# Rotary embedding turned in place in PSUM for the first three tiles of a decoder layer

## The chip, the cores and the metric

The kernel runs on one core of one Trainium2 chip. The metric is the device time of one execution in microseconds (us), smaller is better. TensorE (PE, with its weight loads as PEld), VectorE (DVE), ScalarE (ACT) and GpSimd (POOL) each run their own queue of instructions; SyncE (SP) issues most of the DMAs. Engines order themselves against each other with semaphores. SBUF holds operands, PSUM (8 banks of 512 float32 in each of 128 partitions) takes the results of TensorE. GpSimd works on SBUF alone in this kernel; VectorE and ScalarE work on both.

## The reference, cut to what matters

One pre-norm decoder layer on x of shape (2, 256, 512): causal self-attention with 32 query heads and 8 key/value heads of size 16, attention over a context, and a ternary feed-forward part. The change touches the rotation of queries and keys:

```python
def _apply_rope(x, cos, sin):
    x1, x2 = jnp.split(x, 2, axis=-1)
    return jnp.concatenate([x1 * c - x2 * s, x1 * s + x2 * c], axis=-1)

x = x + attn(layernorm(x))     # q = rope((x @ Wq) heads), k = rope((x @ Wk) heads), v = x @ Wv
x = x + cross_attn(layernorm(x), ctx)
x = x + bitlinear_ffn(layernorm(x))
```

## The kernel before, in words

The 512 tokens are four tiles t = 0..3 of 128 (two per batch element). For each tile TensorE multiplies the normalised, transposed tile with the joined weights: 512 columns of queries (e = 0) and 256 columns of keys and values (e = 1), each into a PSUM bank: `qkv_bank(t, e)` (L215) is banks 1, 2 for tile 0, banks 3, 4 for tile 1, banks 7, 4 for tile 2. Tile 3 is done later, among the attention steps, and goes through an SBUF place (`proj_place`, L365).

The attention scores are made from operands split into a high part (float32r, rounded by the write) and a low part (what is left over). So for each tile and each e:

- `rotate(t, e)` (L795, VectorE): L812 multiplies the projection with cos into the SBUF tensor `roped`; for e = 1, L815 copies the values to `vaug`; L819, twice, multiplies the swapped halves with the signed sin into `rope_tmp`; L823 adds `rope_tmp` to `roped`. The increment of `rope_read` on the second L819 is also what tells TensorE that the bank is free.
- `heads_high(t, e)` (L555, ScalarE, L565 for queries and L569 for keys): rounds `roped` into `stk`, twice per head.
- `heads_low(t, e)` (L825, VectorE, L832 and L835): `roped` minus the high part into `stk`.
- `stack_T` (L1152, TensorE, L1156): transposes `stk` in 5 stacks of 4 transposes per tile; the results for the tiles 0 and 1 go to banks 5, 1, 6, 2 in turn (`ST_BANKS`), so stack 1 overwrites the queries of tile 0 and stack 3 its keys. ScalarE copies them out (L576).

The order on each engine is written out by hand. VectorE (L862 to L883): low part of the transposed tile 1 (L841), rotate(0,0), a small shift for tile 3 (`mean_shift(3)`, L851), rotate(0,1), the low parts of tile 0, `tile_low(2)`, rotate(1,0), rotate(1,1), `tile_low(3)`, the low parts of tile 1, a small product (L876), rotate(2,0), rotate(2,1), low parts of tile 2, then the attention loop (L1067). ScalarE (L723 to L742): ..., `tile_T(1)`, heads_high(0,0), `normalise(3)` (L716), heads_high(0,1), tile_T(2), tile_T(3), copies of the stacks 0 to 4, heads_high(1, ...), copies of the stacks 5 to 9, heads_high(2, ...). TensorE (L1341 to L1357): the projections of tiles 0 and 1, the last passes of tile 1 with the low part of the weights (L1144), `tile_T(3)` (L1110, needs normalise(3)), stacks(0), the queries of tile 2, stacks(1), the keys of tile 2. GpSimd makes the low part of the weights meanwhile (L496, two SBUF inputs, four instructions) and then a chain of products for the context attention (L513, L515, L518).

From about 29 us the loop over 16 groups of heads runs (L1479 on TensorE, L1067 on VectorE): scores by query into banks 0, 1, 2, maxima on VectorE in place in PSUM (L1003), transposed maxima, scores by key, exp, causal select on GpSimd (L535), weighted values. Side work is put between by the table `BESIDE` (L285): "rot", "hi", "lo", "st" of tile 3, "whole" (L406, scaling of the feed-forward weights, shared by GpSimd and VectorE), "a" (L1205, L662 and L983) and so on.

## Time and profile before

| | |
|---|---|
| median of 3 runs | 230.72 us (230.19 to 231.79) |
| the profiled execution | 231.82 us, of which the span of the trace is 230.1 us |
| mean granted TensorE clock | 0.989 of full speed |
| PE busy | 213.2 us (93%) |
| DVE busy | 155.3 us (67%) |
| ACT busy | 124.8 us (54%) |
| POOL busy | 59.7 us (26%) |

The busy shares are taken over the whole span. In the first 35 us all five engines take part in one chain; in the feed-forward part at the end TensorE alone is nearly always busy. The page's fourth section gives the chain that ended last 67% on PE, 16% on DVE and 9% on ACT.

### The profile page before, as it was taken

What the parts mean: (1) busy time and instruction counts of PE and PEld (TensorE: products, weight loads), DVE (VectorE), ACT (ScalarE), POOL (GpSimd) and SP (SyncE); (2) the same over time, 40 slices, a digit from 0 to 9 for tenths busy, and PEclk for the clock granted to TensorE, in tenths of its full rate; (3) what the DMA queues carried; (4) which work ended last, traced back from release to release, by engine and by line L of the source; (5) the groups of instructions that cost most, each with busy time, mean ns of one, the idle gap of its engine ahead of it and who ended that gap; (6) DMA issues with size and microseconds to landing.
All of it is one profiled execution on the core that took longest, in us unless ns stands there. A gap on an engine that the chain in (4) does not pass through costs nothing.

```text
span 230.1 us, 4338 instructions
## 1 busy us (share of the span) xinstructions
PE 213.2 (93%) x1492; PEld 153.6 (67%) x1500; DVE 155.3 (67%) x567; ACT 124.8 (54%) x210; POOL 59.7 (26%) x76
## 2 busy tenths in 40 slices
PE   8898989979988899999899997999999999999993
PEld 3377867656765567456764544888987878767771
DVE  2489988997896897599922658888655675353233
ACT  2638768766699755558695645726524124322320
POOL 4499920473222438432201060000000010000000
PEclk9999999997999999999999999999999999999998
DMA  6999400000652121453701180000000000020002
GB/s 177 372 401 413 161 1 1 4 2 1 209 185 104 47 53 46 137 183 97 252 12 49 33 333 0 3 0 3 0 1 0 3 0 0 3 91 0 3 0 93
DMA packets 9079, 19.98 MB, mean 87 GB/s; under 512 B 1153, under 2 KB 1537, under 8 KB 9057
## 3 DMA queue, kind: packets, MB, share of 16 engines
q1 hardware_dynamic: 8480, 19.60, 24.4%
q8 instruction: 12, 0.20, 0.4%
q10 hardware_dynamic: 576, 0.10, 0.2%
q14 instruction: 11, 0.08, 0.1%
HBM read 18.58 MB, written 1.05 MB: 85 GB/s over the span
## 4 chain that ended last, share of the span: by engine, by line
PE 67%; DVE 16%; ACT 9%; issue 6%; DVEq 0%; POOL 0%; ACTq 0%; POOLq 0%
PE ps L1314 14%; PE ps L1177 10%; PE ps L1329 8%; DVE ps L1003 4%; PE ps L1205 4%; PE ps L1267 3%; PE ps L1236 3%; PE ps L1283 3%; PE ps L1338 3%; PE ps L1156 3%; PE ps L1110 2%; PE ps L1377 2%; PE ps L1459 2%; PE ps L1388 2%; PE ps L1418 2%
## 5 line engine op out<-in xcount | busy, mean ns | idle before, releaser
L1003 DVE CUSTOM_DVE_ANT_0 ps<-ps,maskf 128x128 f32<-128x128 f32 (+1 forms) x128 | 41.1, 392 | 1.1 <-PE ps L1388 0.9
L535 POOL TENSOR_SCALAR_AFFINE_SELECT prob<-prob 128x512 f32<-128x512 f32 x32 | 20.6, 666 | 67.5 <-ACT prob L750 67.5
L750 ACT ACTIVATE prob<-ps 128x1536 f32<-128x1536 f32 x16 | 23.3, 1453 | 20.1 <-PE ps L1424 20.1
L620 ACT CAST in_hi<-inter 128x256 f16<-128x256 f32 (+1 forms) x22 | 8.9, 405 | 24.0 <-DVE inter L956 24.0
L485 POOL TENSOR_TENSOR rstd<-veps,neghalf 128x1 f32<-128x1 f32 x12 | 6.6, 552 | 57.2 <-DVE veps L785 57.2
L1314 PE MATMUL ps<-h_hi,gate_q 128*128 128x256 f16 (+1 forms) x88 | 20.4, 273 | 0.0
L1314 PE MATMUL ps<-h_hi,up_q 128*128 128x256 f16 (+1 forms) x88 | 20.4, 273 | 0.0
L1314 PE MATMUL ps<-h_lo,up_q 128*128 128x256 f16 (+1 forms) x88 | 20.4, 272 | 0.0
L1314 PE MATMUL ps<-h_lo,gate_q 128*128 128x256 f16 (+1 forms) x88 | 20.4, 272 | 0.0
L956 DVE TENSOR_TENSOR inter<-gate_s,ps 128x256 f32<-128x256 f32 (+1 forms) x22 | 9.2, 419 | 14.8 <-PE ps L1314 14.3
L1003 DVE DVE_READ_ACCUMULATOR2_ANT mx<- 128x1 f32 x128 | 17.9, 140 | 0.0
L1329 PE MATMUL ps<-wqkv,in_lo 128*128 128x512 bf16 (+1 forms) x44 | 16.7, 379 | 0.8 <-DVE x L966 0.5
L613 ACT ACTIVATE gate_s<-ps 128x256 f32<-128x256 f32 (+1 forms) x22 | 8.4, 381 | 16.1 <-PE ps L1314 16.0
L1205 PE MATMUL ps<-xwk,xwq 128*128 128x256 f32 x64 | 16.2, 396 | 0.1
L959 DVE TENSOR_TENSOR in_lo<-inter,in_hi 128x256 f16<-128x256 f32 (+1 forms) x22 | 9.3, 425 | 10.4 <-ACT in_hi L620 10.4
L1205 PEld LDWEIGHTS ps<-xwk,xwq 128*128 128x128 f32 x64 | 11.7, 194 | 3.1 <-issue 1.1
L1329 PE MATMUL ps<-wqkv,in_hi 128*128 128x512 bf16 (+1 forms) x36 | 13.6, 379 | 0.0
L1377 PE MATMUL ps<-ksT,qsT 64*128 64x128 f32 x64 | 10.8, 289 | 3.0 <-DVE amat_lo L983 2.2
L1377 PEld LDWEIGHTS ps<-ksT,qsT 64*128 64x128 f32 x64 | 8.6, 188 | 6.6 <-issue 5.8
L1388 PE MATMUL ps<-ksT,qsT 64*128 64x256 f32 x64 | 12.3, 306 | 0.5 <-DVE mT L1073 0.3
L1156 PE MATMUL ps<-ident,stk 128*128 128x128 f32 x80 | 11.3, 278 | 1.2 <-ACT up_q L638 0.7
L1418 PE MATMUL ps<-qsT,ksT 64*128 64x512 f32 x32 | 11.7, 446 | 0.0
(185 smaller groups left out, 546.6 us busy)
## 6 DMA issues: line engine op xcount, KB each, us to landing
raw<-gate_dram SPq DMA_DIRECT2D x1, 2752.0 KB, 17.2
raw<-up_dram SPq DMA_DIRECT2D x4, 688.0 KB, 5.0
wqkv<-wqkv_dram SPq DMA_DIRECT2D x4, 384.0 KB, 6.1
raw<-down_dram SPq DMA_DIRECT2D x2, 768.0 KB, 4.7
x<-x_dram SPq DMA_DIRECT2D x4, 256.0 KB, 5.6
xwq<-xwq_dram SPq DMA_DIRECT2D x1, 1024.0 KB, 8.9
xwk<-xwk_dram SPq DMA_DIRECT2D x1, 1024.0 KB, 11.1
wo<-wo_dram SPq DMA_DIRECT2D x1, 1024.0 KB, 18.0
```

The lines of the kernel that those rows point to most:

```text
L535: nc.gpsimd.affine_select(out=v, in_=v, compare_op=ALU.is_ge, fill=0.0, base=0, pattern=[[0, GROUP], [1, P]], channel_multiplier=-1).then_ ...
L750: nc.scalar.activation(prob[:, i % 2, :], ps[:, 3:6, :].rearrange("p a b -> p (a b)"), ACT.Exp, scale=DH ** -0.5).then_inc(exp_done, 1)
L959: nc.vector.tensor_tensor(in_lo[0:r, n % 3, :], inter[0:r, n % 2, :], in_hi[0:r, n % 3, :], ALU.subtract).then_inc(in_lo_ready, 1)
L1003: nc.vector.tensor_tensor_reduce(scores, scores, mask, 1.0, LOWEST, ALU.add, ALU.max, to).then_inc(max_done, 1)
L1156: mm = nc.tensor.transpose(to[:, a * P:(a + 1) * P], stk[:, t % 2, h:h + 2, :, :].rearrange("p h c d -> p (h c d)"), ident[:, :])
L1177: mm = nc.tensor.matmul(to, lhs(k), rhs(k), start=(k == 0 and n == 0), stop=(k == KD - 1 and n == 2))
L1205: mm = nc.tensor.matmul(to[:, 0:T], xwq[:, k, m * P:(m + 1) * P], xwk[:, k, half * T:(half + 1) * T], start=(k == 0), stop=(k == KD - 1))
L1314: mm = nc.tensor.matmul(ps[0:r, where + n % 2, 0:T], w[:, k, cols], h[:, k, b * T:(b + 1) * T], start=(k == 0 and h is h_hi), stop=(k == K ...
L1329: mm = nc.tensor.matmul(bank(4 + q), half[0:r, n % 3, q * P:(q + 1) * P], down_q[0:r, it * D:(it + 1) * D], start=(it == 0 and half is in_hi),
L1377: nc.tensor.matmul(ps[:, 0, h * P:(h + 1) * P], qsT[b][rows, 4 * gp + h, 0:P], ksT[rows, gp, b * T:b * T + P], start=True, stop=True).then ...
L1388: nc.tensor.matmul(ps[:, 1 + h // 2, (h % 2) * T:(h % 2 + 1) * T], qsT[b][rows, 4 * gp + h, P:T], ksT[rows, gp, b * T:(b + 1) * T], start= ...
L1418: nc.tensor.matmul(bank(3 + n), ksT[rows, gp, b * T:b * T + P], qsT[b][rows, 4 * gp + 2 * n:4 * gp + 2 * n + 2, :], start=True, stop=True)
```

## The change

For the tiles 0 to 2 the projection is no longer moved to `roped`. VectorE first makes the two sin products into `rope_tmp` (SBUF), then multiplies the projection with cos in place in its PSUM bank, then adds `rope_tmp` in place in the bank. ScalarE rounds the high parts and VectorE takes the low parts from the bank. Tile 3 does the same in `proj_place`, in SBUF. The copy of the values comes after the cos product. The semaphore `rope_read` is gone: a bank is free once the low part is taken (`lo_ready`), and a new semaphore `turned` orders VectorE's own steps, with a wait before the cos product and one before the sum (before: one, ahead of the sum). The wait for an old `roped` buffer (`hi_ready`, t >= 2) is gone.

```diff
@@ -184,8 +184,8 @@
...
         w_high, w_low_done = sem("w_high"), sem("w_low_done")
-        qkv_ps, rope_read, roped_ready, v_sb = (
-            sem("qkv_ps"), sem("rope_read"), sem("roped_ready"), sem("v_sb"))
+        qkv_ps, turned, roped_ready, v_sb = (
+            sem("qkv_ps"), sem("turned"), sem("roped_ready"), sem("v_sb"))
         hi_ready, lo_ready = sem("hi_ready"), sem("lo_ready")
@@ -363,6 +363,12 @@
...
         proj_place = up_q[:, :, :].rearrange("p a b -> p (a b)").bitcast(F32)[:, 0:QK]
+
+        def rotated(t, e):
+
+            columns = slice(0, D) if e == 0 else slice(D, QK)
+            place = proj_place[:, columns] if t >= EARLY else qkv_bank(t, e)[:, 0:QK - D if e else D]
+            return place.rearrange("p (h d) -> p h d", d=DH)
@@ -559,15 +565,15 @@
...
                     act.wait_ge(stack_set, 4)
-                r = roped[:, t % 2, :].rearrange("p (h d) -> p h d", d=DH)
+                r = rotated(t, e)
                 s = stk[:, t % 2, :, :, :].bitcast(F32R)
...
                     nc.scalar.copy(s[:, 0:HEADS, 1:3, :],
-                                   r[:, 0:HEADS, :].unsqueeze(2).broadcast_to([P, HEADS, 2, DH])
+                                   r.unsqueeze(2).broadcast_to([P, HEADS, 2, DH])
                                    ).then_inc(hi_ready, 1)
...
                     nc.scalar.copy(s[:, HEADS:, 1:4:2, :],
-                                   r[:, HEADS:, :].unsqueeze(2).broadcast_to([P, KV, 2, DH])
+                                   r.unsqueeze(2).broadcast_to([P, KV, 2, DH])
                                    ).then_inc(hi_ready, 1)
@@ -584,7 +590,7 @@
...
                 if w == 1 and c == 0:
-                    act.wait_ge(rope_read, 2 * TT)
+                    act.wait_ge(lo_ready, 2 * TT)
                 nc.scalar.activation(tern_target(w)[0:rows, at:at + n], raw[0:rows, at:at + n], ACT.Abs,
@@ -803,36 +809,35 @@
...
                     src = proj_place[:, lo * DH:hi * DH]
-                if t >= 2:
-                    dve.wait_ge(hi_ready, 2 * (t - 2) + e + 1)
-                to = roped[:, t % 2, lo * DH:hi * DH]
+                src = src[:, 0:nh * DH]
                 tmp = rope_tmp[:, lo * DH:hi * DH]
-                halves = src[:, 0:nh * DH].rearrange("p (h e d) -> p h e d", e=2, d=DH // 2)
+                halves = src.rearrange("p (h e d) -> p h e d", e=2, d=DH // 2)
                 cos = rope[:, t % 2, 0, :].unsqueeze(1).broadcast_to([P, nh, DH])
-                nc.vector.tensor_tensor(to.rearrange("p (h d) -> p h d", d=DH),
-                                        src[:, 0:nh * DH].rearrange("p (h d) -> p h d", d=DH), cos, ALU.mult)
-                if e == 1 and t < EARLY:
-                    nc.vector.tensor_copy(vaug[:, t, :, 0:DH], src[:, nh * DH:nh * DH + KV * DH].rearrange(
-                        "p (h d) -> p h d", h=KV)).then_inc(v_sb, 1)
                 for half in range(2):
...
                                                   halves[:, :, 1 - half, :], sin, ALU.mult)
-                ins.then_inc(rope_read, 1)
-                dve.wait_ge(rope_read, 2 * t + e + 1)
-                nc.vector.tensor_tensor(to, to, tmp, ALU.add).then_inc(roped_ready, 1)
+                ins.then_inc(turned, 1)
+                dve.wait_ge(turned, 4 * t + 2 * e + 1)
+                heads = src.rearrange("p (h d) -> p h d", d=DH)
+                nc.vector.tensor_tensor(heads, heads, cos, ALU.mult).then_inc(turned, 1)
+                if e == 1 and t < EARLY:
+                    nc.vector.tensor_copy(vaug[:, t, :, 0:DH], qkv_bank(t, e)[:, nh * DH:nh * DH + KV * DH].rearrange(
+                        "p (h d) -> p h d", h=KV)).then_inc(v_sb, 1)
+                dve.wait_ge(turned, 4 * t + 2 * e + 2)
+                nc.vector.tensor_tensor(src, src, tmp, ALU.add).then_inc(roped_ready, 1)
...
                 dve.wait_ge(hi_ready, 2 * t + e + 1)
-                r = roped[:, t % 2, :].rearrange("p (h d) -> p h d", d=DH)
+                r = rotated(t, e)
                 s = stk[:, t % 2, :, :, :]
...
                 if e == 0:
-                    nc.vector.tensor_tensor(w[:, 0:HEADS, 3, :], r[:, 0:HEADS, :], s[:, 0:HEADS, 1, :],
+                    nc.vector.tensor_tensor(w[:, 0:HEADS, 3, :], r, s[:, 0:HEADS, 1, :],
                                             ALU.subtract).then_inc(lo_ready, 1)
                 else:
-                    nc.vector.tensor_tensor(w[:, HEADS:, 2, :], r[:, HEADS:, :], s[:, HEADS:, 1, :],
+                    nc.vector.tensor_tensor(w[:, HEADS:, 2, :], r, s[:, HEADS:, 1, :],
                                             ALU.subtract).then_inc(lo_ready, 1)
@@ -1163,9 +1168,8 @@
...
                     if s in (1, 3):
-                        pe.wait_ge(rope_read, 2)
                         pe.wait_ge(v_sb, 1)
-                    pe.wait_ge(lo_ready, 2 * t + 1 + (s % NST) // (NST - 1))
+                    pe.wait_ge(lo_ready, 2 if s == 3 else 2 * t + 1 + (s % NST) // (NST - 1))
                     if s >= len(ST_BANKS):
@@ -1352,14 +1356,14 @@
...
             stacks(1)
-            pe.wait_ge(rope_read, 4)
+            pe.wait_ge(lo_ready, 4)
             pe.wait_ge(v_sb, 2)
...
                     pe.wait_ge(xnT_low, TT - 1)
-                    pe.wait_ge(rope_read, 2)
+                    pe.wait_ge(lo_ready, 2)
                     pe.wait_ge(v_sb, 1)
@@ -1407,7 +1411,7 @@
...
                 if i == 0:
-                    pe.wait_ge(rope_read, 2 * EARLY)
+                    pe.wait_ge(lo_ready, 2 * EARLY)
                     pe.wait_ge(v_sb, EARLY)
```

## Rows read from the trace of the kernel before

**Rows 1.** Busy time by stretch: stretch, its length, each engine's busy us (instructions), granted clock

```profile
15.47:18.31 2.84, 2.84 (x20) 2.52 (x19) 2.84 (x2) 0.00 (x0) 2.84 (x4) 1.00 1.04 416
19.21:20.16 0.95, 0.00 (x1) 0.00 (x1) 0.90 (x2) 0.95 (x3) 0.95 (x2) 1.00 1.00 411
49.31:50.75 1.44, 0.00 (x1) 0.03 (x1) 1.44 (x4) 0.68 (x1) 0.83 (x1) 1.00 0.00 0
51.10:54.50 3.40, 3.40 (x28) 2.24 (x26) 2.80 (x19) 2.18 (x4) 0.66 (x2) 0.50 0.01 1
...
57.20:62.70 5.50, 5.26 (x46) 4.09 (x47) 4.96 (x25) 3.21 (x6) 1.22 (x2) 1.00 0.53 174
```

**Rows 2.** The chain that ended last, 11 to 31 us: start us, us, what

```profile
19.30 0.82 ACT xn L716
...
20.16 0.66 PE ps L1110 x4
20.82 2.37 PE ps L1156 x20
...
26.00 2.24 PE ps L1156 x20
```

**Rows 3.** VectorE in order of time: start us, us, line, out<-in, count

```profile
14.09 0.68 DVE L812 TENSOR_TENSOR roped<-ps,rope 128x512 f32<-128x512 f32 x1
14.69 0.75 DVE L819 TENSOR_TENSOR rope_tmp<-ps,rope 128x256 f32<-128x256 f32 x2
15.47 2.84 DVE L823 TENSOR_TENSOR roped<-roped,rope_tmp 128x512 f32<-128x512 f32 x1
...
22.90 0.69 DVE L823 TENSOR_TENSOR roped<-roped,rope_tmp 128x512 f32<-128x512 f32 x1
...
25.70 1.37 DVE L835 TENSOR_TENSOR stk<-roped,stk 128x128 fp32r<-128x128 f32 x1
```

**Rows 4.** GpSimd in order of time, the same columns

```profile
14.07 3.68 POOL L496 TENSOR_TENSOR w_lo<-wqkv,qsT 128x768 fp32r<-128x768 f32 x2
...
21.64 1.29 POOL L518 TENSOR_TENSOR bkq<-bkq,oT 128x512 f32<-128x512 f32 x1
...
25.11 1.81 POOL L518 TENSOR_TENSOR bkq<-bkq,oT 128x512 f32<-128x512 f32 x1
```

**Rows 5.** ScalarE in order of time, the same columns

```profile
18.34 1.05 ACT L565 CAST stk<-roped 128x1024 fp32r<-128x1024 f32 x1 [4.89 <-DVE roped L823]
```

**Rows 6.** VectorE by line and shape, 0 to 52 us: busy us, mean ns

```profile
L1003 DVE CUSTOM_DVE_ANT_0 ps<-ps,maskf 128x256 f32<-128x256 f32 x16 | 6.4, 459 | 0.0
...
L983 DVE TENSOR_TENSOR amat_lo<-ps,xnT_r 128x256 fp32r<-128x256 f32 x2 | 0.8, 417 | 0.4 <-ACT xnT_r L662 0.4
```

**Rows 7.** The chain that ended last, 34 to 52 us

```profile
50.20 0.42 DVE amat_lo L983
```

**Rows 8.** VectorE in order of time, 47 to 49 us

```profile
47.07 0.59 DVE L812 TENSOR_TENSOR roped<-up_q,rope 128x128 f32<-128x128 f32 x1
47.58 0.65 DVE L819 TENSOR_TENSOR rope_tmp<-up_q,rope 128x64 f32<-128x64 f32 x1
...
48.85 1.42 DVE L823 TENSOR_TENSOR roped<-roped,rope_tmp 128x128 f32<-128x128 f32 x1
```

**Rows 9.** GpSimd in order of time, 46 to 50 us

```profile
46.11 1.41 POOL L406 TENSOR_SCALAR raw<-raw,inv 128x1376 f32<-128x1376 f32 x1
...
47.48 0.68 POOL L535 TENSOR_SCALAR_AFFINE_SELECT prob<-prob 128x512 f32<-128x512 f32 x1
...
48.11 0.63 POOL L535 TENSOR_SCALAR_AFFINE_SELECT prob<-prob 128x512 f32<-128x512 f32 x1
48.73 1.41 POOL L406 TENSOR_SCALAR raw<-raw,inv 128x1376 f32<-128x1376 f32 x1
```

**Rows 10.** VectorE in order of time, 18 to 20 us

```profile
18.36 0.28 DVE L812 TENSOR_TENSOR roped<-ps,rope 128x128 f32<-128x128 f32 x1
...
19.12 0.29 DVE L823 TENSOR_TENSOR roped<-roped,rope_tmp 128x128 f32<-128x128 f32 x1
```

## The prediction, made before the changed kernel was run

> **What bounds the kernel now.** I read the table of busy time by stretch first, then the chain of waits, then the queues of VectorE, GpSimd and ScalarE side by side. The table shows a stretch of 2.84 us (15.47 to 18.31) in which VectorE has two instructions, ScalarE none at all, and TensorE still has work; a little later, 19.21 to 20.16, TensorE stands still for 0.95 us [rows 1]. The chain goes through both: the sum of rotate(0,0), then the normalisation of tile 3 on ScalarE, then TensorE's transpose of tile 3 at 20.16 and the stacks [rows 2]. Side by side the queues say why: the sum L823 on 512 columns takes 2.84 us at 15.47 and 0.69 us at 22.90 [rows 3]. During the long one GpSimd runs two L496 without a break, from 14.07 to 17.75 [rows 4]; 18.31 - 17.75 = 0.56 us is the sum's own work, so it made no headway before GpSimd stopped. Both read two tensors from SBUF. The cos and sin products at 14.09 and 14.69, with one input in PSUM, ran at 0.68 us and 0.75 us (for two) in the same GpSimd stretch [rows 3]. It comes again: L835, two SBUF inputs, takes 1.37 us at 25.70 where 128 columns take some 0.29 us [rows 3, 10]; GpSimd's L518 runs 25.11 to 26.92, and is itself 0.52 us over its 1.29 us because L832 came first [rows 4].
>
> The Trainium skill says this of it (SBUF — State Buffer, "Who interferes with whom"): a VectorE instruction with two SBUF inputs and a GpSimd instruction that reads SBUF lock each other out for a whole instruction, and one with at most one SBUF input does not contend. By that rule the trace agrees, with the 2.84 us beside 0.69 us above.
>
> **What is removed.** In the tiles 0 to 2 the sums and the low parts get one input from PSUM, so these stalls go: 2.84 - 0.69 = 2.15 us at 15.47 and 1.37 - 0.29 = 1.08 us at 25.70. Neither is worth its size on the path.
>
> The first. Rotate(0,0) becomes two sin products 0.75, cos product 0.68, sum 0.69, and 0.03 us at each of two waits (14.69 + 0.75 = 15.44, next start 15.47 [rows 3]): 14.09 + 2.18 = 16.27 us instead of 18.31. Then ScalarE's high part, 1.05 us [rows 5], and the normalisation, 0.82 us [rows 2]: tile 3 is normalised at about 18.2 us. But TensorE works until 19.21 on the last passes of tile 1, whose weights come from the same GpSimd instructions [rows 1], and these gain nothing. So of 2.0 us the path gets the 0.95 us in which TensorE stood still. Next due are the stacks: they need the low part of tile 0's queries, at about 17.4 + 0.7 = 18.1 us, and transpose 3 first, so TensorE decides and not they. A small part comes on top: in the chain the first 20 stack transposes take 2.37 us and the next, which do not wait for tile_low(2), 2.24 us [rows 2]. I take 0.1 us.
>
> The second, 1.08 us at 25.70, holds back rotate(2,0). Its result is wanted by ScalarE only after the stack copies of tile 1, and the keys of tile 2, which TensorE finishes later, decide when VectorE may start on the maxima. I cost it at nothing; the cover is over 1 us of TensorE's projection of those keys. If the cover were gone it would be worth up to 1.08 us, the lower bound of the range takes that in.
>
> **What is added.** One more wait per rotation. Before, the products overlapped (14.09 to 14.69 is 0.60 us for a 0.68 us instruction); now the cos product starts only when the sin products are through. That is 0.03 + 0.08, about 0.1 us each, eight times. Six lie before VectorE becomes the bound and are covered by the 2.0 us. The two of tile 3 lie on the path (the chain is VectorE's from 36 to 50 us): 0.1 us for the first; the second is hidden in the stall below, bound 0 to 0.1 us.
>
> In-place operation in PSUM with two inputs is nowhere shown for this line. Nearest: the maxima L1003, in place in PSUM, 459 ns for 256 columns, and L983, PSUM and SBUF into SBUF, 417 ns [rows 6]. So in place costs between nothing and 0.04 us per 256 columns, 0.08 us for 512; I take nothing, since 1 us of slack on VectorE hides six of these at either price. ScalarE reading its high part from PSUM: between 0 and 0.1 us of the 1.05, either way hidden by the same 1 us.
>
> The other page on this speaks against the change: VectorE: DVE Perf Modes, "The TRN2 errata", gives a VectorE instruction with a PSUM source 62 cycles more than one with an SBUF source, an estimate of 0.06 us each at its 0.96 GHz. The trace shows the opposite of a difference: 0.68 us from PSUM (L812) and 0.69 us from SBUF (L823 at 22.90) [rows 3]. By the page some 12 instructions would cost 0.8 us of VectorE, all under the slack, and the sum would be the same.
>
> Banks are held longer. Stack 3 now waits for both low parts of tile 0. The second is short behind the first (keys: 0.28 us for the product to 0.29 us for the sum [rows 10]) and behind ScalarE's normalisation; by my walk it is ready near 18.8 us, and stack 3 is due near 21.2. Bank 4 for tile 2's keys waits for the low part of tile 1's keys, which the tenth stack ahead of it in TensorE's queue waits for anyway. Cost nothing, with over 2 us of cover on the first. The waits on all eight low parts ahead of the up-weights come tens of us after their release.
>
> **The stall that stays.** Tile 3 is rotated in SBUF, before and after. At 47 us VectorE's four operations alternate with GpSimd's queue: L812 waits for the end of a L406 at 47.52, the first sin product (0.65 us for 64 columns) for a select until 48.16, the second for the next select, and the sum, 1.42 us, for a third L406 until 50.14 [rows 8, 9]. The next step in the chain starts at 50.20 [rows 7]; TensorE has nothing from 49.31 to 50.75, and then runs at a granted clock of 0.50 (1.2 GHz) for 3.4 us, 51.1 to 54.5 [rows 1]. That costs about 1 us: the step from 50.75 to 57.21 takes 6.46 us, the next, of nearly the same content, 5.5 us [rows 1]. In the new order it is again four operations in the same place, sin, sin, cos, sum. What decides is whether two sin products slip in between a L406 and a select. The nearest row is the pair itself: after the first select, one 64-column product got in and the second lost to the next select. So I take that the pattern stays, and the sum ends where it does now, within 0.05 us.
>
> **The sum**, against the profiled execution of 231.82 us (span 230.1): -0.95 - 0.1 + 0.1 + 0.0 = -0.95 us, so 230.87. It lies 1.10 us over the median of the runs, which the forecast is to be compared with: 230.72 - 0.95 = 229.8 us. From 50 us on nothing hangs on absolute time, the loads being issued behind the same steps, so I let the gain pass through to the end.
>
> **Rivals.**
>
> 1. *The stall at 47 us breaks too.* If the two sin products pass in one gap (64 columns instead of 128 end earlier), the sum comes before the third L406 and rotate(3,1) ends near 49.0 instead of 50.27: 1.3 us, no gap of 1.44 us on TensorE and, if the clock then holds, 1 us more. 229.8 - 2.3 = 227.5 us. For it: the margins are below 0.1 us. Against: the pair row above. Chance 0.23.
>
> 2. *The gain is given back.* The shifted work meets one more stretch at half clock (1 us as above) or the steps of the loop fall differently: 230.7 us. For it: the one stretch is set off by a gap that small shifts could make elsewhere; against: the 0.95 us gap did not lower the clock (1.00 in both rows), and gaps shrink. Chance 0.14.
>
> 3. *The change doesn't do what it says*: a sum in PSUM with one SBUF input is still held up by GpSimd. Then all stays, plus 0.2 us of added waits: 230.9 us. The products at 14.09 and 14.69 speak against it. Chance 0.04.
>
> 4. *Slower.* The added wait in the rotation of tile 3 lengthens TensorE's gap and with it the half clock in the loop. Every us of TensorE work at half clock costs about 1/3.4 = 0.3 us, so it decides against the 0.95 us gain only when over 3.2 us more are run so; at twice that, 229.8 + 1.9 = 231.7 us. Against it: the added time is 0.1 us on a gap of 1.44 us. Chance 0.07.
>
> The forecast itself has 0.52.
>
> **How the numbers follow.** 1% is 2.3 us, about what a measurement of this kernel tells from no change. Only rival 1 (227.5) and the lower edge of my own case pass 228.4: faster 0.23 + 0.02 = 0.25. Slower by over 1% means over 233.0 us, twice rival 4's loss: 0.05 of its 0.07. The rest is 0.70. The range reaches from rival 1 less 0.2 us, 227.3, to rivals 2 and 3 and a run's scatter, 231.1; the likeliest case alone is 229.0 to 230.5, the lower end with the 1.08 us above partly on the path, the upper with in-place costs and the waits of tile 3.
>
> **What would show it.** L823 at about 15.6 us at 0.7 us; L835 of tile 1 at 0.3 us; TensorE without its 0.95 us gap; the transpose of tile 3 near 19.3; the first maxima, L1003, about 1 us earlier than now; the sum of rotate(3,1) still 1.4 us and the half clock near 50 to 54. The forecast is wrong if the last two are gone, if GpSimd's L496 now take longer than 1.84 us each, or if a new low-clock stretch appears.

## The result: 229.61 us, and the profile of the changed kernel

| | before | changed |
|---|---|---|
| median (18 runs each) | 230.59 us | 229.61 us (228.49 to 230.25) |
| ratio, with its 95% interval | | 0.9949 (0.9931 to 0.9966) |
| the profiled execution, and its span | 231.82, 230.1 us | 229.55, 227.8 us |
| mean granted TensorE clock in it | 0.989 | 1.00 |

(One of the 18 runs of before was 533.26 us, the others 229.72 to 231.94; the median is not moved by it.) The change saves 1.0 us by the medians and 1.2 us by the ratio, whose interval is 0.8 to 1.6 us. The forecast was 0.95 us. Lines have moved: the sin products are L818, the cos product L823, the sum L828, the low parts L837 and L840, the dot product ahead of tile 2's rotation (L876 before) L881, the maxima L1008, the transposes of tile 3 L1115, the stacks L1161, the scores L1381.

VectorE of the changed kernel in order of time (start us, us, line, out<-in):

```profile
14.16 0.75 DVE L818 TENSOR_TENSOR rope_tmp<-ps,rope 128x256 f32<-128x256 f32 x2
14.94 0.70 DVE L823 TENSOR_TENSOR ps<-ps,rope 128x512 f32<-128x512 f32 x1
15.67 0.70 DVE L828 TENSOR_TENSOR ps<-ps,rope_tmp 128x512 f32<-128x512 f32 x1
...
24.31 0.28 DVE L840 TENSOR_TENSOR stk<-ps,stk 128x128 fp32r<-128x128 f32 x1
24.51 1.20 DVE L881 CUSTOM_DVE_ANT_0 stat<-bqk 128x4 f32<-128x4 f32 x1
```

GpSimd and ScalarE in the same stretch:

```profile
14.14 3.68 POOL L502 TENSOR_TENSOR w_lo<-wqkv,qsT 128x768 fp32r<-128x768 f32 x2
...
24.42 1.28 POOL L524 TENSOR_TENSOR bkq<-bkq,oT 128x512 f32<-128x512 f32 x1
```

```profile
16.41 1.02 ACT L571 CAST stk<-ps 128x1024 fp32r<-128x1024 f32 x1 [2.89 <-DVE ps L828]
17.31 0.82 ACT L722 ACTIVATE xn<-x,shift,rstd 128x512 f32<-128x512 f32 x1
```

GpSimd's two products take 3.68 us as before [rows 4], but the sum inside them now takes 0.70 us where it took 2.84 us [rows 3]. Rotate(0,0) ends at 16.37 us. The stall of 1.08 us at the low part L835 is gone too, but the dot product behind it, whose two inputs lie in SBUF, takes 1.20 us in place of 0.15 us: the stall moved to the next instruction with two SBUF inputs.

The chain that ended last, 17 to 29 us (start us, us, what):

```profile
17.86 1.39 PE ps L1149 x8
19.24 0.44 PE ps L1115 x4
19.68 2.18 PE ps L1161 x20
...
24.67 2.18 PE ps L1161 x20
...
28.25 0.63 PE ps L1381 x4
```

It is TensorE's alone from 8.75 us to the first scores, where before it went through VectorE's sum and ScalarE's normalisation [rows 2]. TensorE has no gap ahead of tile 3. Busy time by stretch (the stretch, its length, the busy us of PE, PEld, VectorE, ScalarE and GpSimd in this order, then the granted clock, the DMA share and GB/s):

```profile
48.12:49.54 1.42, 0.00 (x1) 0.03 (x1) 1.42 (x4) 0.67 (x1) 0.80 (x1) 1.00 0.00 0
49.54:55.02 5.48, 4.91 (x44) 3.62 (x44) 4.65 (x23) 3.17 (x6) 1.22 (x2) 1.00 0.00 1
56.00:61.50 5.50, 5.25 (x48) 4.10 (x46) 5.01 (x23) 3.87 (x5) 1.22 (x2) 1.00 0.67 238
```

The gap of TensorE ahead of 50 us is still there, 1.42 us for 1.44 [rows 1]. In this execution the half clock did not follow it: the step behind it took 5.48 us, at a granted clock of 1.00, where before it took 6.46 us. So the two profiles differ by more than the change: 230.1 - 227.8 = 2.3 us of span, of which 50.75 - 49.54 = 1.21 us was gained by 50 us, 6.46 - 5.48 = 0.98 us is the half-clock stretch, and 0.1 us lies later. The experiments must say whether that 0.98 us belongs to the change. The two traces start alike: GpSimd's pair of products begins at 14.07 us in one and at 14.14 us in the other.

### The profile page after: what moved, and what is told of

Same layout as the page of the kernel before. It is cut to its first block, busy times and chain, and to the rows that moved or that the text cites. A ratio compares the mean times of both kernels' runs of the same rounds, so it can differ in the third digit from the quotient of the medians.

```text
span 227.8 us, 4334 instructions
## 1 busy us (share of the span) xinstructions
PE 211.5 (93%) x1492; PEld 152.6 (67%) x1500; DVE 153.7 (67%) x567; ACT 124.7 (55%) x210; POOL 57.5 (25%) x76
## 3 DMA queue, kind: packets, MB, share of 16 engines
HBM read 18.58 MB, written 1.05 MB: 86 GB/s over the span
## 4 chain that ended last, share of the span: by engine, by line
PE 70%; DVE 16%; ACT 7%; issue 6%; DVEq 0%; POOL 0%; ACTq 0%; POOLq 0%
PE ps L1318 14%; PE ps L1181 10%; PE ps L1333 8%; DVE ps L1008 5%; PE ps L1271 3%; PE ps L1240 3%; PE ps L1287 3%; PE ps L1342 3%; PE ps L1161 3%; PE ps L1209 3%; PE ps L1115 3%; PE ps L1130 2%; PE ps L1381 2%; ACT prob L756 2%; PE ps L1140 2%
## 5 line engine op out<-in xcount | busy, mean ns | idle before, releaser
L1008 DVE CUSTOM_DVE_ANT_0 ps<-ps,maskf 128x128 f32<-128x128 f32 (+1 forms) x128 | 41.1, 392 | 0.7 <-PE ps L1392 0.6
L541 POOL TENSOR_SCALAR_AFFINE_SELECT prob<-prob 128x512 f32<-128x512 f32 x32 | 20.0, 649 | 67.2 <-ACT prob L756 67.2
L1008 DVE DVE_READ_ACCUMULATOR2_ANT mx<- 128x1 f32 x128 | 17.9, 140 | 0.0
L1381 PE MATMUL ps<-ksT,qsT 64*128 64x128 f32 x64 | 10.6, 285 | 2.8 <-DVE amat_lo L988 1.9
L1381 PEld LDWEIGHTS ps<-ksT,qsT 64*128 64x128 f32 x64 | 8.5, 186 | 6.3 <-issue 5.7
L1161 PE MATMUL ps<-ident,stk 128*128 128x128 f32 x80 | 11.1, 277 | 1.7 <-ACT up_q L644 0.7
L412 POOL TENSOR_SCALAR raw<-raw,inv 128x1376 f32<-128x1376 f32 (+1 forms) x8 | 11.2, 1407 | 1.8 <-DVE inv L896 1.8
```

The lines of the kernel that those rows point to most:

```text
L412: unit.tensor_scalar(v, v, inv[0:rows, w:w + 1], ROUND, ALU.mult, ALU.add).then_inc(pool_whole if unit is nc.gpsimd else dve_whole, 1)
L541: nc.gpsimd.affine_select(out=v, in_=v, compare_op=ALU.is_ge, fill=0.0, base=0, pattern=[[0, GROUP], [1, P]], channel_multiplier=-1).then_ ...
L1008: nc.vector.tensor_tensor_reduce(scores, scores, mask, 1.0, LOWEST, ALU.add, ALU.max, to).then_inc(max_done, 1)
L1161: mm = nc.tensor.transpose(to[:, a * P:(a + 1) * P], stk[:, t % 2, h:h + 2, :, :].rearrange("p h c d -> p (h c d)"), ident[:, :])
L1381: nc.tensor.matmul(ps[:, 0, h * P:(h + 1) * P], qsT[b][rows, 4 * gp + h, 0:P], ksT[rows, gp, b * T:b * T + P], start=True, stop=True).then ...
```

## The experiments

Theory A, that of the forecast: the sum of rotate(0,0) is what counts, 0.95 us and a little more, because TensorE is next; the rest of the change costs and brings nothing. Theory B: the half clock behind 50 us is part of the effect. Theory C: the gain comes from other places of the change (low parts, rotations of tile 1, the later release of the banks). Unless told otherwise, ratios are to the kernel before on the same chip, with their 95% interval; that kernel's median is 231.15 us (35 runs) beside experiments 1 to 4, 231.01 (22) beside 5 to 8, 230.63 (25) beside 9 to 12, which are three chips. For each execution the mean granted clock is known too. The profiled ones with a half-clock stretch of some 3.5 us have 0.989 to 0.993, so executions at 0.994 or less are counted as having one, and the others are called executions at full clock. At full clock the kernel before has 230.81, 230.79 and 230.33 us on the three chips.

### 1. The kernel before, unchanged

> The kernel before, unchanged, beside itself. Theory (the stretch at half clock near 51 us comes and goes from run to run and costs about 1 us): the runs fall in two groups about 1 us apart, near 230.3 and 231.5 us, and those with the longer time show a mean clock near 0.99, the others 1.00; ratio 1.000 within 0.003. Rival (the stretch belongs to every run of this kernel, and its end is what the change won): all runs near 231 us at a clock of 0.99.

231.64 us (230.05 to 232.64), ratio 1.0004 (0.9970 to 1.0037); 8 of the 12 executions have the lower mean clock. Its profile shows another course than the one that the prediction was made from. VectorE and GpSimd:

```profile
14.75 0.75 DVE L819 TENSOR_TENSOR rope_tmp<-ps,rope 128x256 f32<-128x256 f32 x2
15.53 1.00 DVE L823 TENSOR_TENSOR roped<-roped,rope_tmp 128x512 f32<-128x512 f32 x1
...
17.35 1.05 DVE L823 TENSOR_TENSOR roped<-roped,rope_tmp 128x128 f32<-128x128 f32 x1
...
22.74 1.08 DVE L823 TENSOR_TENSOR roped<-roped,rope_tmp 128x128 f32<-128x128 f32 x1
```

```profile
14.13 1.86 POOL L496 TENSOR_TENSOR w_lo<-wqkv,qsT 128x768 fp32r<-128x768 f32 x1
15.94 2.31 POOL L496 TENSOR_TENSOR w_lo<-wqkv,qsT 128x768 fp32r<-128x768 f32 x1
```

The sum starts 15.53 - 14.13 = 1.40 us behind GpSimd's pair, exactly as in the first profile (15.47 - 14.07 [rows 3, 4]). There it waited for the end of the pair and took 2.84 us. Here it took 1.00 us, of which 0.56 us are its own work (as in the prediction), so it waited 0.44 us, until 15.97 us. That is the seam of the pair (14.13 + 1.86 = 15.99 us). At the seam the waiting sum was let in, and GpSimd's second product took 2.31 us for the 1.86 us of the first. In the first profile the sum had waited as long when the seam came, and GpSimd's second product was let in ahead of it: the same encounter at the same distance, won by the other side. TensorE has no gap ahead of tile 3 here. Instead two sums of 128 columns are held up, in rotate(0,1) and in rotate(1,1), and VectorE reaches the low part of tile 1 too late for TensorE:

```profile
19.10 0.60 PE L1110 MATMUL ps<-ident,xn 128*128 128x128 f32 x4
...
25.07 0.66 PE L1156 MATMUL ps<-ident,stk 128*128 128x128 f32 x4 [0.38 <-DVE stk L832]
```

The stacks of tile 1 start at 25.07 us; in the changed kernel they start at 24.51 us. So 0.56 us are lost here, where the first profile lost 1.3 us (it starts them at 25.84). The hold-ups of this execution share that cost: in the profile of experiment 4 the sum of rotate(1,1) is held up as long (1.07 us, at 22.17), but VectorE is 0.57 us further on by then, and the stacks of tile 1 start at 24.50 us without a gap. The gap at 50 us is there (1.43 us) and the clock stays at 1.00 behind it. Of the 35 executions beside experiments 1 to 4, 19 have the lower mean clock, with a median of 232.08 us against 230.81 for the others: 1.3 us. The stalls and the half clock are events that this program has in some executions and not in others. Of all the profiles, five have this sum with two SBUF inputs. It was let in at the seam in two of them (here, and in experiment 3, where it starts 1.75 us behind the pair) and passed over in three (1.40 us behind in the first profile, 1.52 in experiment 7, 1.59 in experiment 11).

### 2. Only rotate(0,0) in PSUM

All else as before; the high and the low part of tile 0's queries are then taken from bank 1. In the kernel before:

```diff
-                nc.vector.tensor_tensor(to.rearrange("p (h d) -> p h d", d=DH),
-                                        src[:, 0:nh * DH].rearrange("p (h d) -> p h d", d=DH), cos, ALU.mult)
+                first = (t, e) == (0, 0)
+                if not first:
+                    nc.vector.tensor_tensor(to.rearrange("p (h d) -> p h d", d=DH),
+                                            src[:, 0:nh * DH].rearrange("p (h d) -> p h d", d=DH), cos, ALU.mult)
...
+                if first:
+                    heads = src.rearrange("p (h d) -> p h d", d=DH)
+                    nc.vector.tensor_tensor(heads, heads, cos, ALU.mult).then_inc(turned, 1)
+                    dve.wait_ge(turned, 1)
+                    to = src
                 nc.vector.tensor_tensor(to, to, tmp, ALU.add).then_inc(roped_ready, 1)
```

> The kernel before, with only the queries of tile 0 rotated in place in their bank; tiles 1 to 3 and the keys of tile 0 go through SBUF as before. Theory (the whole gain is the stall of the first sum): the sum at 15.6 us takes 0.7 us, TensorE has no gap ahead of the transpose of tile 3, and all of the gain is there, -1.2 us, 229.4. Rival (the second stall, in tile 1's low part, is worth something too): part of the gain, -0.6 us or less.

230.37 us (229.27 to 231.16), ratio 0.9940 (0.9909 to 0.9972). The six executions at full clock have a median of 229.61 us, 1.2 us under the 230.81 us of the kernel before beside them; the changed kernel gains 1.3 us in this comparison (experiment 5). Theory A gets what it expects: one of the six early rotations brings the whole.

### 3. All but rotate(0,0)

The changed kernel, with rotate(0,0) through `roped` in SBUF and in the old order.

```diff
             place = proj_place[:, columns] if t >= EARLY else qkv_bank(t, e)[:, 0:QK - D if e else D]
+            if (t, e) == (0, 0):
+                place = roped[:, 0, 0:D]
...
```

> The changed kernel, with the queries of tile 0 rotated through SBUF as before, all else as changed. Theory (the first sum is all): the sum takes 2.8 us again, the gap of 0.95 us on TensorE is back, and the time is that of the kernel before, 230.6 us, ratio 1.000 or up to 0.001 above for the added waits of tile 3. Rival (second stall counts): 0.4 us or more stay won, 230.1 us.

230.98 us (229.08 to 233.83), ratio 0.9966 (0.9932 to 1.0001). The profiled execution does not show the sum at 2.8 us that was expected. VectorE was let in at the seam (GpSimd's second product takes 2.36 us), and its next instruction with two SBUF inputs met the pair instead:

```profile
15.64 0.69 DVE L836 TENSOR_TENSOR roped<-roped,rope_tmp 128x512 f32<-128x512 f32 x1
...
17.45 1.16 DVE L845 TENSOR_TENSOR stk<-roped,stk 128x512 fp32r<-128x512 f32 x1
```

```profile
15.70 2.36 POOL L504 TENSOR_TENSOR w_lo<-wqkv,qsT 128x768 fp32r<-128x768 f32 x1
```

Times from 229.08 us (all of the gain) to above 231 us (none) lie in one set of runs. By the ratios the intervals of experiments 2 and 3 overlap. At full clock they part: the eight executions here have a median of 230.98 us (two at 229.08 and 229.71, six from 230.87 to 231.34), against 230.81 us for the kernel before and 229.61 us in experiment 2 (229.27 to 230.12). At the median the rest of the change brings nothing, which speaks for A and against C. That the two fast executions are ones in which the sum was let in at the seam fits the profiled one, whose TensorE has no gap from 17 to 31 us, but it isn't shown: that one is neither of the two, and an early beginning (experiment 11) would make an execution fast too.

### 4. One operand moved: the sin products of rotate(0,0) in an idle bank

The kernel before; the sum then reads `roped` in SBUF and the sin products in PSUM, and writes to SBUF. No in-place work, no new wait, no bank held longer.

```diff
-                tmp = rope_tmp[:, lo * DH:hi * DH]
+                tmp = bank(7) if (t, e) == (0, 0) else rope_tmp[:, lo * DH:hi * DH]
```

> The kernel before, order of the operations and banks' release as before, but the two sin products of tile 0's queries go to the unused bank 7 instead of SBUF, so that the sum has one input in PSUM. Theory (what holds the sum up is its second SBUF input while GpSimd reads SBUF): the sum takes 0.7 us, -1.2 us, 229.4, as with the rotation in place, 0.1 us earlier for want of the added wait. Rival (it is the order of operations or the destination in PSUM that frees it): the sum still takes 2.8 us, 230.6 us.

230.09 us (229.12 to 233.12), ratio 0.9944 (0.9910 to 0.9978). VectorE and GpSimd:

```profile
15.48 0.69 DVE L823 TENSOR_TENSOR roped<-roped,ps 128x512 f32<-128x512 f32 x1
```

```profile
14.00 3.69 POOL L496 TENSOR_TENSOR w_lo<-wqkv,qsT 128x768 fp32r<-128x768 f32 x2
```

One input out of SBUF is enough. The sum runs at its full speed inside GpSimd's pair, and neither is lengthened. It brings what the whole change brings, at full clock too (229.70 against 230.81 us). The Trainium skill (SBUF — State Buffer, "Who interferes with whom") says that a VectorE instruction with at most one SBUF input does not contend with GpSimd, and the trace agrees: 0.69 us beside 2.84 us. The Trainium skill also says there that whoever issues first gets the shared ports for the whole instruction. Inside one instruction the trace agrees (the sum waits 0.44 us for the seam in experiment 1). At the seam it doesn't: in the first profile the sum starts at 15.47 us and GpSimd's second product at 15.89 us, and yet the sum was passed over and took 2.84 us.

### 5. The changed kernel again

> The changed kernel, unchanged, beside the kernel before on this chip. Theory (in the kernel before, which of GpSimd and VectorE gets the SBUF reads first differs from run to run, and the change takes VectorE out of it up to 31 us): ratio 0.995 (0.993 to 0.997), a smaller spread of its runs than before's; in its trace the three sums and the three low parts of queries take 0.70 us each, the first query score starts at 28.3 us. Rival (the change works only on the one stalled sum seen in the first trace): the ratio is that of the kernel with the first sum alone in place, 0.994, and the spread is that of before.

229.85 us (229.25 to 232.12), ratio 0.9941 (0.9908 to 0.9974). Here the half clock is back, behind a gap of the same length:

```profile
48.77 0.29 PE L1381 MATMUL ps<-ksT,qsT 64*128 64x128 f32 x1 [1.41 <-DVE amat_lo L988]
```

```profile
45.00:50.00 5.00, 3.48 (x24) 2.59 (x23) 4.58 (x14) 3.13 (x5) 3.15 (x4) 0.97 0.00 0
50.00:55.00 5.00, 5.00 (x32) 3.37 (x31) 3.50 (x16) 3.05 (x6) 1.22 (x2) 0.69 0.00 1
```

(The last three columns are the granted clock, the DMA share and GB/s.) Four of the 11 executions have the lower mean clock, none of the 18 of the first comparison, 10 of 22 of the kernel before on this chip. The four take 230.71 us, the others 229.49, which is 1.3 us under the 230.79 us that the kernel before has at full clock on this chip. So the gain is there without the half clock, and the change doesn't take the half clock away. Whether it makes it rarer these counts don't say: it is 10 of 22 against 4 of 11 on one chip. Theory B falls as the explanation of the gain, and stays as a cost of its own, about 1.2 us in such an execution. The smaller spread that was expected isn't there: 2.9 us, as for the kernel before (230.42 to 233.30).

### 6 and 7. Taking the stall at 47 us away, with the change and without it

The stall comes from a piece of GpSimd's work, ("whole", 0, 2), that stands beside the rotation of tile 3. In both kernels it goes one step later:

```diff
-            ([("whole", 0, 2)], [("st", 13), ("tern", 0, 0)], [("rot", 3, 1), ("a", 0, 1), ("tern", 0, 1)]),
-            ([("st", 14)], [("hi", 3, 1), ("lo", 3, 0)], [("a", 1, 0), ("st", 15), ("lo", 3, 1)]),
+            ([], [("st", 13), ("tern", 0, 0)], [("rot", 3, 1), ("a", 0, 1), ("tern", 0, 1)]),
+            ([("st", 14), ("whole", 0, 2)], [("hi", 3, 1), ("lo", 3, 0)], [("a", 1, 0), ("st", 15), ("lo", 3, 1)]),
```

> The changed kernel, with GpSimd's scaling of the third quarter of the gate weights moved one loop step later, so that it no longer runs while VectorE rotates the keys of tile 3. Theory (the last sum, 1.38 us near 47.7, waits for this instruction, and TensorE's gap of 1.4 us behind it sets off the half clock in some runs): the sum takes 0.3 us, TensorE's gap falls to 0.3 us or less, no run shows a mean clock of 0.993 or less, and the time falls by 1.1 to 1.6 us against the changed kernel, 228.3 us. Rival (the scaling is needed where it stands, by the ternary rounding on ScalarE, or meets another VectorE instruction later): no more than 0.3 us are won.

> The kernel before with the same move of GpSimd's scaling, nothing else. Theory: the stall of tile 3's keys and the half clock go, 1.1 to 1.6 us less than before, but the stalls of the tiles 0 to 2 stay, so it ends about 1.1 us above the changed kernel with the same move: ratio 0.994. Rival (the two gains are the same one, namely the half clock, and do not add): this kernel and the changed one with the move end within 0.3 us of each other.

With the change: 228.38 us (228.00 to 228.81), ratio 0.9862 (0.9817 to 0.9907), none of 6 executions at the lower clock. Without it: 229.78 us (228.78 to 231.23), ratio 0.9926 (0.9893 to 0.9959), 3 of 12 at the lower clock. TensorE with the change, then VectorE and GpSimd:

```profile
48.42 0.29 PE L1381 MATMUL ps<-ksT,qsT 64*128 64x128 f32 x1 [0.33 <-DVE amat_lo L988]
```

```profile
45.84 1.12 DVE L818 TENSOR_TENSOR rope_tmp<-up_q,rope 128x64 f32<-128x64 f32 x2
47.00 0.62 DVE L823 TENSOR_TENSOR up_q<-up_q,rope 128x128 f32<-128x128 f32 x1
47.65 0.29 DVE L828 TENSOR_TENSOR up_q<-up_q,rope_tmp 128x128 f32<-128x128 f32 x1
```

```profile
52.23 1.84 POOL L412 TENSOR_SCALAR raw<-raw,inv 128x1376 f32<-128x1376 f32 x1
```

The sum of rotate(3,1) takes 0.29 us in place of 1.38 us, the gap is 0.33 us in place of 1.42 us, and the piece itself costs TensorE nothing where it now stands: it takes 1.84 us there for 1.45, and TensorE's gap nearby is 0.48 us for 0.49 before the move. With the change, 229.85 - 228.38 = 1.5 us is gained on the same chip: 1.42 - 0.33 = 1.1 us from the gap, and the rest fits 4 in 11 executions times 1.2 us for the half clock. At full clock alone the move gains 229.49 - 228.38 = 1.1 us with the change and 230.79 - 229.72 = 1.1 us without it. The two edits add up: 1.2 us (231.01 - 229.78) for the one alone, 1.2 us (231.01 - 229.85) for the other, 2.6 us (231.01 - 228.38) for both. Experiment 7 ends 1.4 us above experiment 6, where 1.1 us was expected.

### 8. Tile 3 in the old order on top

The version of experiment 6; tile 3 goes through `roped` again, cos first, with one wait per rotation.

```diff
-            place = proj_place[:, columns] if t >= EARLY else qkv_bank(t, e)[:, 0:QK - D if e else D]
+            place = roped[:, 1, columns] if t >= EARLY else qkv_bank(t, e)[:, 0:QK - D if e else D]
```

> The changed kernel with GpSimd's scaling one step later, and tile 3 rotated in the old order through SBUF, with one wait per rotation instead of two. Theory (an added wait costs 0.1 us where VectorE sets the pace): the rotation of tile 3's queries takes 1.99 us again instead of 2.11, 0.1 to 0.2 us less than with the move alone: ratio 0.989 to 0.990. Rival (the wait is hidden by TensorE): no difference to the move alone.

228.30 us (228.24 to 228.48), ratio 0.9861 (0.9821 to 0.9901), none of 6 at the lower clock. From the start of rotate(3,0) to that of VectorE's next instruction it is 36.95 to 38.93 = 1.98 us, in place of 37.05 to 39.16 = 2.11 us in the changed kernel, so the second wait costs 0.13 us where it stands. The median is 0.08 us under experiment 6, less than these runs resolve.

### 9 and 10. How much slack the first rotation has

The version of experiment 8, with one or three more cos products of 512 columns, whose results nobody uses, ahead of rotate(0,0); the edit for one, where three have `[0:3]`:

```diff
+                for spare in ((ubc[:, :], roped[:, 0, 0:D], roped[:, 1, 0:D])[0:1] if (t, e) == (0, 0) else ()):
+                    nc.vector.tensor_tensor(spare.rearrange("p (h d) -> p h d", d=DH),
+                                            src.rearrange("p (h d) -> p h d", d=DH), cos, ALU.mult)
```

> The kernel with the move and the old order for tile 3 (228.3 us), with one more cos product of 512 columns, into an unused place, ahead of the rotation of tile 0's queries on VectorE: 0.6 us more there. Theory (of the 2 us won by VectorE only about 1 lies on TensorE's path, the rest is slack): no change, 228.3 us, TensorE still without a gap ahead of the transpose of tile 3. Rival (VectorE's chain itself sets the pace from there on): 0.6 us more, 228.9.

> The same with three more products, 1.8 us on VectorE. Theory: 1.8 - 0.95 us of slack = 0.85 us of gap on TensorE ahead of the transpose of tile 3, and 0.9 to 1.2 us more at the end, 229.3. Rival (VectorE's chain sets the pace): 1.8 us more, 230.1.

Each product adds 0.6 us to VectorE. One more: 228.53 us (228.07 to 230.09), ratio 0.9919 (0.9890 to 0.9947); its 7 executions at full clock have 228.40 us. Experiment 8 has 228.30, but ran on another chip; on this one the nearest is experiment 12 with 228.46 us in its three executions at full clock, and the profile with one more product has no TensorE gap ahead of tile 3. So it costs nothing that these runs resolve. Three more: 229.59 us (228.68 to 230.40), ratio 0.9936 (0.9906 to 0.9967), none at the lower clock, 1.2 us over one more at full clock. TensorE waits for the normalisation again:

```profile
18.92 0.66 PE L1124 MATMUL ps<-ident,xn 128*128 128x128 f32 x4 [0.74 <-ACT xn L722]
```

So 1.8 - 0.74 = 1.06 us of slack stand behind the sum, as the prediction's 1 us says, and past it VectorE's time goes to the end. Three of the 10 executions with one more product had the lower mean clock although the gap at 48 us is only 0.32 us there; the one profiled has no such stretch.

### 11. The stall put back alone

The version of experiment 8, with rotate(0,0) through SBUF.

```diff
+            if (t, e) == (0, 0):
+                place = roped[:, 0, 0:D]
```

> The same best kernel with the queries of tile 0 rotated through SBUF in the old order. Theory (which engine reads first differs from run to run at one and the same distance of their starts): the runs spread again, between 228.2 us, the sum not held up, and 229.5 us, the sum at 2.8 us, against 0.3 us of spread without it. Rival (a stall of fixed length): all runs at 229.4 us.

229.70 us (228.69 to 230.68), ratio 0.9946 (0.9907 to 0.9986). The profiled execution has the stall and the gap behind it (VectorE, GpSimd and TensorE):

```profile
14.56 2.67 DVE L836 TENSOR_TENSOR roped<-roped,rope_tmp 128x512 f32<-128x512 f32 x1
```

```profile
12.97 3.71 POOL L504 TENSOR_TENSOR w_lo<-wqkv,qsT 128x768 fp32r<-128x768 f32 x2
```

```profile
19.08 0.65 PE L1123 MATMUL ps<-ident,xn 128*128 128x128 f32 x4 [0.81 <-ACT xn L724]
```

The ten executions lie at 228.69, 228.71, 228.97, 228.99, then 229.58 to 230.06 (four), then 230.65 and 230.68 with the lower clock. The eight at full clock have a median of 229.29 us, 0.9 us over the 228.40 us of experiment 9 on the same chip, which has one product more on VectorE but the operand in PSUM. So the stall alone is worth about 0.9 us here.

The spread doesn't say in which executions the sum was held up. The profiled one has the stall in full and is the fastest of the ten (228.69 us). Its beginning is early instead: the eight warm-up matmuls that TensorE runs first take 5.21 us, against 6.57 us in the first profile of the changed kernel, and GpSimd's pair starts at 12.97 us, against 13.94 us in experiment 8.

```profile
1.08 5.21 PE L1350 MATMUL ps<-ones 128*128 128x512 f32 x8 [1.08 <-POOL ones L487]
```

The profiled execution of experiment 10, the fastest of its ten too, has the same early beginning (12.89 us). So the beginning of the program can move a single execution by up to about 1 us, as much as the stall does, and it is a rival for any spread of that size.

### 12. The stall that moved to the dot product

The version of experiment 8; the dot product stands behind rotate(2,1) in place of ahead of rotate(2,0).

```diff
-            nc.vector.tensor_tensor_reduce(stat[:, 0, 0:KD], bqk[:, 0, :], bqk[:, 1, :], 1.0, 0.0,
-                                           ALU.mult, ALU.add, dotp[:, :]).then_inc(dot_ready, 1)
             rotate(2, 0)
             rotate(2, 1)
+            nc.vector.tensor_tensor_reduce(stat[:, 0, 0:KD], bqk[:, 0, :], bqk[:, 1, :], 1.0, 0.0,
+                                           ALU.mult, ALU.add, dotp[:, :]).then_inc(dot_ready, 1)
```

> The best kernel with the small product of the biases moved behind the rotations of tile 2, out of GpSimd's way: it reads two SBUF tensors and takes 1.1 us near 24.5 instead of 0.15, and holds up the rotation of tile 2's queries. Theory (that rotation has more than 1 us of cover): no change, 228.3 us within 0.1. Rival (the stall only moved from tile 1's low part to here and still costs): 0.5 to 0.9 us less.

228.54 us (228.11 to 229.50, 4 runs), ratio 0.9898 (0.9846 to 0.9949): no gain over the 228.30 us of experiment 8 or the 228.40 us of experiment 9 at full clock. VectorE:

```profile
25.78 0.70 DVE L834 TENSOR_TENSOR ps<-ps,rope_tmp 128x512 f32<-128x512 f32 x1
27.85 0.36 DVE L823 TENSOR_TENSOR rope_tmp<-ps,rope 128x64 f32<-128x64 f32 x2 [1.37 <-PE ps L1155]
...
28.85 0.15 DVE L889 CUSTOM_DVE_ANT_0 stat<-bqk 128x4 f32<-128x4 f32 x1
```

The dot product takes 0.15 us again, and the time saved turns into a longer wait for tile 2's keys: 1.37 us, where the changed kernel waits 0.41 us. The stall in that place costs nothing.

This profile, with a mean clock of 0.993, also has a half-clock stretch in another place than near 50 us. TensorE's last gap ahead of it is 0.68 us long, and then the busy times by stretch, in the order given above, are:

```profile
32.59 0.66 PE L1167 MATMUL ps<-ident,stk 128*128 128x128 f32 x4 [0.68 <-ACT up_q L644]
```

```profile
34.80:38.20 3.40, 3.40 (x17) 3.33 (x18) 3.37 (x16) 0.85 (x4) 0.00 (x0) 0.51 0.01 1
```

The same gap of 0.68 us stands in the profiles of both kernels and of experiments 6 and 8, with a granted clock of 1.00 behind it.

## Why the prediction was right, point by point

- **Rotate(0,0).** Forecast: four operations ending at 16.27 us, tile 3 normalised at about 18.2 us. Measured: 16.37 us, of which 0.07 us is this trace's later start (14.16 for 14.09), and 17.31 + 0.82 = 18.13 us. Right.
- **What is next.** Forecast: TensorE, at 19.21 us, so 0.95 us of 2.0. The mechanism was right, and the slack behind it was tested (experiments 9 and 10). The size was under-read. The transposes started 20.16 - 19.08 = 1.08 us earlier, and 1.15 us with the trace's offset. The rest is in the chain's rows: 0.66 us for the four transposes behind the gap [rows 2], 0.44 us without one. Here the idle stretch cost its own length and 0.2 us more, in which the first instructions behind it don't overlap with earlier ones.
- **The stacks.** Forecast 0.1 us, from 2.37 against 2.24 us [rows 2]. Measured 2.18 us in both places, so 0.19 and 0.06 us. The terms -0.95 - 0.1 were -1.15 - 0.25, and the chain agrees within 0.03 us: at the scores TensorE was 29.62 - 28.25 = 1.37 us earlier in the chain.
- **The added wait.** Forecast 0.1 us for the rotation of tile 3's queries. Measured 2.11 us against 1.99 us before: 0.12 us. Right, and the second lies in the stall. Sum at 50 us: -1.21 us measured against -0.95.
- **In place in PSUM, high parts from PSUM, banks held longer: nothing.** 0.70 us for 512 columns with PSUM at both ends, 0.69 from SBUF; ScalarE's high part 1.02 for 1.05 us; the stacks follow one another without a wait for a bank. Right. The Trainium skill's 62 cycles more for a PSUM source (VectorE: DVE Perf Modes, "The TRN2 errata"), an estimate of 0.06 us, don't show: between these two rows lie 0.01 us.
- **The second stall, 1.08 us at 25.70, worth nothing.** For that place right: the stall only moved to the dot product, and taking it from there brings nothing (experiment 12). But the list of stalls was taken from one execution as if it were the program's. In another execution of the same kernel it is the sums of rotate(0,1) and rotate(1,1), and with the 0.44 us that the first sum waits they cost 0.56 us (experiment 1). The change removes these too, which the forecast had nowhere. The measured 1.0 to 1.2 us stands for executions that lost more, less or elsewhere (1.2 us by 50 us against the first profile, 0.5 us against that of experiment 1), and that it lies so near 0.95 us is partly luck.
- **The stall at 47 us stays, with 1.4 us.** Measured 1.38 us, between the same pieces of GpSimd's work. Right; the pair row decided it. **The half clock behind it** was forecast to stay: it did in experiment 5 and not in the first profile. The forecast took an event of some executions (19 of 35) for a fixed one. That did no harm only because both kernels have it. It also read the gain from one profile, 1.10 us over the median, and took it off the median as it stood.
- **The first rival,** the break of that stall, was priced at 1.3 us for the gap and 1 us for the clock. Brought about in experiment 6 it gave 1.1 us, and 0.98 us in an execution that would have had the half clock, but only 0.4 us of it in the mean. **The second** (gain given back), **third** (the sum still held up) and **fourth** (longer half clock) didn't come. The fourth's 0.05 for a time over 233.0 us didn't follow from its own working, which ends at 231.7 us.

The fastest kernel of the study is that of experiment 8, 228.30 us, 1.4% under the kernel before and, on the same chip, 0.7% under the changed one (229.85 us); experiment 6 is the same within what can be measured.

## What to carry to other kernels

When VectorE and GpSimd both read two tensors from SBUF, look for the instruction whose duration differs between two places with one shape, and move one operand of it to PSUM: here a single operand of a single sum brought as much as the rewritten rotation. What it is worth is not the stall but the gap of the engine that is next, and in this kernel 0.2 us more for the overlap lost behind that gap. And take a second profile of the kernel before pricing stalls: those that hang on two engines meeting come and go between executions of one program, so their price is a mean. Before a spread of times is read as such a stall, compare where the first instructions of the profiles start.

## What the runs showed of the hardware that was not expected

- Two GpSimd products in a row do not always shut VectorE out to their end. At one distance of starts, 1.40 us into the pair, VectorE's sum with two SBUF inputs took 2.84 us in one execution (it was let in behind the second product) and 1.00 us in another (let in at the seam, and the second product took 2.31 us for 1.86). In all, VectorE was let in at the seam in two profiles of five. What decides there stays open.
- A TensorE gap of 1.41 to 1.44 us near 49 us was followed by a half-clock (1.2 GHz) stretch in three of the seven profiles that have it (the first of the kernel before, experiments 3 and 5) and not in the other four, in both kernels. The step behind it takes 6.46 us with it and 5.48 us without. With the gap at 0.3 us, 12 of 12 executions with the change had none (experiments 6 and 8), but 3 of 12 of experiment 7, 3 of 10 of experiment 9, 2 of 10 of experiment 11 and 1 of 4 of experiment 12 had a lower mean clock. So this place isn't the only one. One other is in the profile of experiment 12, 34.8 to 38.2 us, behind a gap of 0.68 us that other profiles have without it. What sets the half clock off in one execution and not in another wasn't found.
- The beginning differs between executions. In the two profiles of the changed kernel the eight warm-up matmuls take 6.57 and 5.77 us and GpSimd's pair starts at 14.14 and 13.37 us; over all profiles, whose kernels are alike up to there, it starts between 12.89 and 14.39 us. Why wasn't found.
